# A four-layer graph network on one core: setup rebuilt, low rows split ahead of the turn, order set anew

## The reference

```python
def reference(x, adj, ...):                       # x: (32, 512, 256)
    x = _layernorm(x + _L0(x, adj, W, a))         # GAT, 1 head:  e = leaky(s1_i + s2_j), mask, softmax, @ h, elu
    x = _layernorm(x + _L1(x, adj, ...))          # 8 heads of 32: softmax(mask(q k^T / sqrt(32))) v, then FFN 256-256-256
    x = _layernorm(x + _L2(x, adj, W, a))         # GAT, 4 heads of 64
    x = _layernorm(x + _L3(x, adj, W1, W2, W3))   # e = leaky((x W1)(x W2)^T), mask, softmax, @ (x W3), relu
    return x
```

## Time and profile before

| | us |
|---|---|
| median of three executions | 3187.53 |
| profiled execution, its own time | 3182.73 |
| span in the profile | 3180.9 |
| PE busy | 2825.5 (89%) |
| ACT busy | 2719.1 (85%) |
| DVE busy | 2656.7 (84%) |
| POOL busy | 2497.8 (79%) |

### The profile page before, as it was taken

How to read it: one execution, slowest core, us unless ns; L and a number is a source line. 1 busy time by engine, 2 the same in 40 slices (tenths; PEclk the granted TensorE clock), 3 DMA queues, 4 the chain that set the end, 5 groups by cost and what they waited for, 6 DMA issues and landing times. The chain is left out here.

```text
span 3180.9 us, 69159 instructions
## 1 busy us (share of the span) xinstructions
PE 2825.5 (89%) x22342; PEld 1541.3 (48%) x22576; DVE 2656.7 (84%) x7357; ACT 2719.1 (85%) x5847; POOL 2497.8 (79%) x2521
## 2 busy tenths in 40 slices
PE   4899998998999999999989999998999999998855
PEld 3444444544555455554545454554454554454433
DVE  4878887988898799889888987988898798898774
ACT  4768888988898998898989879898898999897874
POOL 5657778878788787888878788887878887886874
PEclk8999999999999999999999999999999999999977
DMA  6435545755656666565656665574765566554454
GB/s 151 94 71 103 126 99 112 141 128 121 130 109 122 120 137 127 124 129 114 125 120 140 124 123 114 120 136 111 140 123 122 109 131 130 117 124 97 101 115 84
DMA packets 1215801, 378.88 MB, mean 119 GB/s; under 512 B 1157712, under 2 KB 1194320, under 8 KB 1215440
## 3 DMA queue, kind: packets, MB, share of 16 engines
q1 hardware_dynamic: 1213616, 373.46, 57.0%
q10 hardware_dynamic: 1824, 0.99, 0.2%
HBM read 21.43 MB, written 16.78 MB: 12 GB/s over the span
## 5 line engine op out<-in xcount | busy, mean ns | idle before, releaser
L855 POOL TENSOR_TENSOR split_r<-prob_r,split_r 128x512 f16<-128x512 f32 x768 | 929.7, 1222 | 219.8 <-DVE split_r L1299 219.8
L1264 DVE CUSTOM_DVE_ANT_0 unused<-bank_ps,neg_mask 128x512 bf16<-128x512 f32 x1024 | 650.2, 683 | 38.0 <-PE bank_ps L1466 34.9
L1531 PE MATMUL bank_ps<-val_r,trans_r 128*128 128x64 f16 (+1 forms) x9216 | 626.0, 221 | 58.6 <-DMA trans_r<-split_r 53.4
L1531 PEld LDWEIGHTS bank_ps<-val_r,trans_r 128*128 128x128 f16 x9216 | 523.4, 98 | 301.9 <-issue 109.4
L1084 ACT ACTIVATE prob_r<-bank_ps 128x512 f32<-128x512 f32 x1024 | 564.6, 597 | 120.9 <-remote 58.9
L1249 DVE CUSTOM_DVE_ANT_0 masked_r<-bank_ps,neg_mask 128x512 f32<-128x512 f32 x768 | 508.4, 681 | 130.7 <-ACT bank_ps L1050 102.6
L1299 DVE CAST split_r<-prob_r 128x512 f16<-128x512 f32 x768 | 537.3, 706 | 93.8 <-ACT prob_r L1062 78.6
L1062 ACT ACTIVATE prob_r<-masked_r,low_r 128x512 f32<-128x512 f32 x768 | 556.6, 734 | 53.0 <-DVE low_r L1249 38.3
L1491 PE MATMUL bank_ps<-prob_r,value_ones 128*64 128x512 f32 (+1 forms) x2048 | 553.9, 610 | 3.6 <-ACT prob_r L1084 2.0
L1482 PE MATMUL bank_ps<-stack 98*128 98x512 f16 x1024 | 394.2, 385 | 67.7 <-DVE low L1264 18.9
L861 POOL TENSOR_TENSOR split_r<-xcur,split_r 128x512 f16<-128x512 f32 x256 | 299.4, 1182 | 141.1 <-ACT split_r L976 140.6
(11 more groups left out here) (144 smaller groups left out, 4873.2 us busy)
## 6 DMA issues: line engine op xcount, KB each, us to landing
stack<-qk SPq DMA_DIRECT2D x384, 128.0 KB, 2.5
xcur<-in_x_dram SPq DMA_DIRECT2D x32, 512.0 KB, 5.0
out_dram<-z SPq DMA_DIRECT2D x32, 512.0 KB, 3.3
trans_r<-split_r SPq DMA_TRANSPOSE x768, 2.8
xt_r<-split_r SPq DMA_TRANSPOSE x320, 2.8
stack<-low_rows SPq DMA_DIRECT2D x128, 4.0 KB
qk<-in_adj_dram SPq DMA_DIRECT2D x1, 1024.0 KB, 8.1
z<-in_L_gnn_W_dram SPq DMA_DIRECT2D x4, 256.0 KB, 9.4
```

What stands on the lines that cost most here:

```text
L855: nc.gpsimd.tensor_tensor(split_r[:, j, 1, :], prob_r[:, i, :], split_r[:, j, 0, :], ALU.subtract).then_inc(lo_done.sem, 1)
L1264: nc.vector.tensor_tensor_reduce(out=unused[:, nth % 2, :], in0=bank_ps[entry("bank", "sq", g, t, b, h)][:], in1=neg_mask[:, b, :], scale= ...
L1531: ins = nc.tensor.matmul(bank[:, at:at + width], trans_r[:, i, pp, jb, :], val(g, layer)[:, vp, jb, cols], start=(n == 0), stop=(n == len( ...
```

## The change

**Setup.** The rows of graphs 0 and 1 are loaded among the first weights, and ACT and POOL split them (the list `EARLY`) ahead of most weights. The staging tiles move to other buffers (`STAGED`, slots 4 and 5, and `qk`), so that graphs 2 and 3 load without a wait. Five weights keep their low part on POOL (`SPLIT_POOL`), four get it on DVE (`SPLIT_DVE`) inside `later_setup`, which DVE runs just ahead of its first `mk`. PE waits for each weight where it is first used.

**Low rows.** `mh` on DVE is now three instructions in a chain of semaphores: the scaling, a cast to fp16, and a subtraction, all 128x16 and from SBUF to SBUF. `mt` turns high and low part together by four fp16 matmuls against an fp16 identity, into a bank of 8x512. `mr` casts all eight rows at once; `ml` is gone.

**Order.** `LATER` has new numbers for all kinds of tasks, and the costs of `mh` (0.22 to 0.45) and `mt` (0.4 to 0.25) in the planner are new.

```diff
-        "add_0": 60, "add_3": 66, "ap_0": 50, "ap_2": -3, "ap_ffn": -51, "bc": 22, "bt": -5, "dp": -40, "dv_2":
+    LATER = {"add_0": 28, "add_1": 13, "add_3": 110, "ap_0": 49, "ap_1": -4, "ap_2": 4, "ap_3": 30, "ap_ffn": -75, "ap_out": 41,
...
-            task(("mh", g, t), 0.22, [("mx", g, t, b, h) for b in range(NB) for h in range(QUAD)])
-            task(("mt", g, t), 0.4, [("mh", g, t)], opens=[("bank", ("mt", g, t))])
-            task(("mr", g, t), 0.49, [("mt", g, t)] + ([("md", g - 1, t)] if g else []))
-            task(("ml", g, t), 0.61, [("mr", g, t)], closes=[("bank", ("mt", g, t))])
-            task(("md", g, t), 1.0, [("ml", g, t), ("stack", g)], lands=2.2)
+            task(("mh", g, t), 0.45, [("mx", g, t, b, h) for b in range(NB) for h in range(QUAD)])
+            task(("mt", g, t), 0.25, [("mh", g, t)], opens=[("bank", ("mt", g, t))])
+            task(("mr", g, t), 0.49, [("mt", g, t)] + ([("md", g - 1, t)] if g else []),
+                 closes=[("bank", ("mt", g, t))])
+            task(("md", g, t), 1.0, [("mr", g, t), ("stack", g)], lands=2.2)
...
+        SPLIT_POOL = ("h0", "h2", "q", "k", "v")
+        SPLIT_DVE = ("f1", "f2", "h3", "g")
+        EARLY = [("x", g, 0, n) for g in range(2) for n in range(CT)]
+        STAGED = (4, 5)
...
             for kind, g, *key in ORDER["sp"]:
                 s = g % SLOTS
+                if (kind, g, *key) == ("xd", 2, 0, 0):
+                    sp.wait_ge(weights_lo, len(SPLIT_POOL))
+                    sp.wait_ge(setup_dve, 1)
+                    for staged_slot in STAGED:
+                        load(staged_slot)
                 if kind == "load":
                     if g >= SLOTS:
                         sp.wait_ge(*added.last((g - SLOTS, 3, p) for p in range(HALF)))
-                    elif g in (1, 2, 3):
-                        sp.wait_ge(weights_lo, W_SPLITS)
-                        sp.wait_ge(setup_dve, 1)
...
+            for _, g, phase, n in EARLY:
+                low_rows_of(g, phase, n)
+            for n, k in enumerate(SPLIT_POOL):
                 eng.wait_ge(weights_hi, n + 1)
                 nc.gpsimd.tensor_tensor(W[k][:, 1], scaled_weight(k), W[k][:, 0], ALU.subtract).then_inc(weights_lo, 1)
...
+                eng.wait_ge(rows_loaded, 80)
+                after(nc.vector.tensor_tensor(rows["fb2"][:], rows["fb2"][:], stage_b1, ALU.add))
+                for n, k in enumerate(SPLIT_DVE):
+                    eng.wait_ge(weights_hi, len(SPLIT_POOL) + n + 1)
+                    ins = nc.vector.tensor_tensor(W[k][:, 1], scaled_weight(k), W[k][:, 0], ALU.subtract)
+                ins.then_inc(setup_dve, 1)
...
                 elif kind == "mk":
                     unit = (g, *key)
+                    if (kind, *unit) == first_mask:
+                        later_setup()
...
                     nc.vector.scalar_tensor_tensor(out=low[s][:, t], in0=low[s][:, t], scalar=LOW_SCALE,
                                                    in1=some_col[:].unsqueeze(2).broadcast_to([P, NB, QUAD]),
-                                                   op0=ALU.mult, op1=ALU.mult).then_inc(low_scaled.sem, 1)
-                elif kind == "ml":
-                    t, = key
-                    dve.wait_ge(*low_rows_done.at(g, t))
-                    nc.vector.tensor_tensor(low_rows[:, 1, t, :], bank_ps[entry("bank", "mt", g, t)][0:QUAD, :],
-                                            low_rows[:, 0, t, :], ALU.subtract).then_inc(low_split.sem, 1)
+                                                   op0=ALU.mult, op1=ALU.mult).then_inc(low_chain, 1)
+                    low_links += 1
+                    dve.wait_ge(low_chain, low_links)
+                    parts = low_parts[s][:, t]
+                    nc.vector.tensor_copy(parts[:, :, 0, :], low[s][:, t]).then_inc(low_chain, 1)
+                    low_links += 1
+                    dve.wait_ge(low_chain, low_links)
+                    nc.vector.tensor_tensor(parts[:, :, 1, :], low[s][:, t], parts[:, :, 0, :],
+                                            ALU.subtract).then_inc(low_scaled.sem, 1)
...
                     for b in range(NB):
-                        ins = nc.tensor.transpose(bank[0:QUAD, b * P:(b + 1) * P], low[s][:, t, b, :], ident32[:])
+                        ins = nc.tensor.matmul(bank[0:2 * QUAD, b * P:(b + 1) * P],
+                                               low_parts[s][:, t, b].rearrange("p a h -> p (a h)"), ident16[:], start=True, stop=True)
```

More of the change, by code:

```diff
@@ L936, in scale_weight, with split_weight, high_rows_of @@
                 return nc.scalar.activation(stage_w[k], stage_w[k], ACT.Copy, scale=WSCALE)
+            def split_weight(k):
+                nc.scalar.copy(W[k][:, 0], scaled_weight(k)).then_inc(weights_hi, 1)
+            def high_rows_of(g, phase, n):
+                if phase == 0:
+                    act.wait_ge(*loaded(g))
+                else:
+                    for p in range(HALF):
+                        act.wait_ge(*applied.at(g, BEFORE_PHASE[phase], p))
+                was = prior("split", "x", g, phase, n)
+                if was is not None:
+                    act.wait_ge(*split_free(was))
+                nc.scalar.copy(cols_of(split_r[:, entry("split", "x", g, phase, n), 0, :]),
+                               rows_of(g, phase, n)).then_inc(rows_hi.sem, 1)
             eng.wait_ge(gat_loaded, 32)
             scale_weight("h0").then_inc(weights_scaled, 1)
-            eng.wait_ge(mh_loaded, 32)
-            scale_weight("h2").then_inc(weights_scaled, 1)
+            for _, g, phase, n in EARLY[:CT]:
+                high_rows_of(g, phase, n)
+            eng.wait_ge(weights_scaled, 1)
+            split_weight("h0")
             eng.wait_ge(dots_turned, 1)
@@ L944, in _ @@
                 nc.scalar.copy(t_tile, bank_ps[half][:].rearrange("p (t c) -> p t c", t=CT)).then_inc(dots_copied, 1)
+            eng.wait_ge(mh_loaded, 32)
+            scale_weight("h2").then_inc(weights_scaled, 1)
+            for _, g, phase, n in EARLY[CT:]:
+                high_rows_of(g, phase, n)
+            eng.wait_ge(weights_scaled, 2)
+            split_weight("h2")
+            eng.wait_ge(gram_done, 1)
+            nc.scalar.activation(stage_g, bank_ps[0][:].rearrange("p (t c) -> p t c", t=CT), ACT.Copy,
+                                 scale=WSCALE).then_inc(weights_scaled, 1)
             eng.wait_ge(qkv_loaded, 48)
@@ L947, in _ @@
                 scale_weight(k).then_inc(weights_scaled, 1)
+            eng.wait_ge(weights_scaled, 6)
+            for k in ("q", "k", "v"):
+                split_weight(k)
             eng.wait_ge(ffn_loaded, 80)
@@ L966, in _ @@
                 if kind == "x_hi":
-                    phase, n = key
-                    if phase == 0:
-                        act.wait_ge(*loaded(g))
-                    else:
-                        for p in range(HALF):
-                            act.wait_ge(*applied.at(g, BEFORE_PHASE[phase], p))
-                    was = prior("split", "x", g, phase, n)
-                    if was is not None:
-                        act.wait_ge(*split_free(was))
-                    nc.scalar.copy(cols_of(split_r[:, entry("split", "x", g, phase, n), 0, :]),
-                                   rows_of(g, phase, n)).then_inc(rows_hi.sem, 1)
+                    if ("x", g, *key) not in EARLY:
+                        high_rows_of(g, *key)
                 elif kind == "xt_hi":
@@ L1408, in _ @@
                     job, n = key
+                    if job != "c0":
+                        pe.wait_ge(weights_lo, 1 if job == "h0" else len(SPLIT_POOL))
+                    if job not in ("c0", "h0"):
+                        pe.wait_ge(setup_dve, 2)
                     for t in range(CT):
```

122 lines of the change are left out of this document (65 added, 57 removed), and 22 rows, old and new, of the table LATER.

## The result

Before and after ran side by side on one chip. The changed kernel takes **3154.78 us** (median of 4, 3148.64 to 3160.15), the kernel before 3185.7 us; the ratio is 0.9907, 95% interval 0.9891 to 0.9924. That is 31 us less, and 2 us from the 3157 that were forecast. The profiled execution took 3153.3 us, its span 3151.5, at a mean granted clock of 0.979 (before 0.969).

The account below looks back on a forecast made before the run. Four engines were taken to hold each other up, PE nearest its limit, so about half of PE savings count. Terms -19 - 11 + 18 - 16 = -28 gave 3155 for the profiled execution, 3157 us as median; range 3112 to 3205.

Parts of the forecast that it names:

- start: Setup: rows loaded early, first mask on DVE at 41 us instead of 60.13, -19 us (ends 13 and 23).
- order: New task order: a quarter of the 62 us in low-clock stretches is gained, -16 us.
- low rows, -11 + 18: Low rows: -11 us from cheaper fp16 turns on PE, +18 us from two more small DVE instructions ahead of `mt`.
- signs that I set down for right: First PE matmul 26 to 33 us, first mask 38 to 44, low-row matmuls 15 to 20, idle 70 to 90, among others.
- The rival by which half of the head start is given back: Start: transposes queue behind loads, late weights drag, order brings nothing; 3183 us, no change; chance 0.15.
- The rival that the rows come no earlier: Start: the DMA queue, not SP's wait, sets the first transpose; given no chance of its own.
- The low rows on PE: 256 fp32 transposes become fp16 matmuls, 17.7 us busy; PE saves 21.5 us, half reaches the end, -11 us.
- The low chain: DVE ahead of `mt`: 36 PE waits grow by 1.0 us each, half counts, +18 us (ends +6 and +80).
- my mark "below 50" for wrong: Idle time ahead of the low-row matmuls (L1534) below 50 us would show the prediction wrong.
- The slower rival: Low chain: POOL holds both new DVE instructions nearly every time, 64 sets grow by 2.0 us; 3217 us, chance 0.2.
- the bare stretch: Every third graph PE holds almost only `sq`, at low clock: 6.9 us each, some nine times, 62 us.
- the rival at 3125 us: Order: the low-clock stretch goes for good, three quarters of 62 us come through; chance 0.2.

Follow-up runs that it names:

- e1: Kernel before with the changed kernel's setup only, order and low rows old: 3173.0 us, ratio 0.9963.
- e8: Changed kernel with the low rows of before, `ml` put into DVE's row behind the planned end of `mr`: 3161.5 us, ratio 0.9924.
- after: The changed kernel itself: new setup, new order, new low rows with 3 links: 3154.8 us, ratio 0.9907.
- e4: Changed kernel with the setup of before, new order and new low rows kept: 3170.0 us, ratio 0.9951.
- e9: Kernel before with ten memsets on POOL ahead of its ninth weight split, to start the first graph late: median up 8.1 us, ratio 1.0024.
- e5: Kernel before with the new low rows cut to one DVE instruction per set, low part of the extremes left zero: 3180.8 us, ratio 0.9987.
- e6: Changed kernel with one DVE instruction per low-row set in place of three, low part of the extremes left zero: 3137.2 us, ratio 0.9853.
- e2: Kernel before with the new low rows (3 links), old setup, old order with `ml` struck out of DVE's row: 3243.7 us, ratio 1.0189.
- e7: Changed kernel with the cast made three times in a chain, so 5 links per set: 3194.6 us, ratio 1.0035.
- e3: Kernel before with new setup and new low rows (3 links), old order with `ml` struck out: 3227.8 us, ratio 1.0135.

## Why the prediction was right in its total, step by step

The total was right, and in part by luck. The split that e1, e8 and after give (setup, then order, then low rows) shows three terms that were each off by 4.5 to 13.7 us, with errors that cancelled:

| step | predicted us | measured on this path us |
|---|---|---|
| start | -19 | -11.5 |
| order | -16 | -11.5 |
| low rows, -11 + 18 | +7 | -6.7 |
| sum | -28 | -29.7 |

The two gains were 12 us smaller than forecast, and the loss that I forecast for the low rows did not come (each step is known to some 4 to 7 us). (The runs of before beside the changed kernel's own had a median of 3185.7 us, which is why the sum here is 29.7 and not 31.) Of the signs that I set down for right, PE's first matmul, the links' maxima and the fewer windows of low clock came. The first mask (45.00), the matmuls' 25.0 us, the links' means and the idle time did not.

**The start.** The turned rows came by the count of bytes: 29.60 us against "about 29". The first mask was forecast at 41 and came at 45.00, since I let `later_setup` begin at 33.5. I had left out that the second `ends` stands behind `val_r` in DVE's row, which waits for ACT until 36.58. I had counted all of it as carried to the end. From e4 to the changed kernel 14.4 us of the mask gave 15.2 of time, in the old order 17.6 gave 11.5 (e1) and 12.1 gave 8.1 (e9). Each of these shares is known to some 0.2 to 0.5, so that the new order carries more than the old is not shown. The rival by which half of the head start is given back and the order brings nothing (3183) fell by its time, but in the old order about a third does go. The rival that the rows come no earlier fell too: PE has them 24 us sooner.

**The low rows on PE.** Sized too high from two neighbours: the matmuls' busy time is 25.0 us and not 17.7, so 14.2 us are saved and not 21.5. The mean of 98 ns for 128 columns is nearer to the 123 of 256 columns than I had taken. Half of 14.2 is 7 us. With the further links removed, this saving and the loss of `ml` together are worth 3.7 us in the old order (before to e5) and 24 us in the new one (e8 to e6). My factor of one half is no constant of the kernel. I gave `ml`'s hop nothing; no run parts it from the matmuls.

**The low chain.** The term of +18 us met what e6 to after gives, +17.5 us, but its working was wrong, and this is luck. "PE already sits idle for this step 36 times, 45.4 us in all" misread the view: 31.5 of these us, 29 times, are idle time of the weight loads, and the matmuls waited 7 times, 13.9 us; the earlier trace rows had the 13.9. I then expected 36 waits to grow by 1.0 us each, to 81 us; it was 40.7, and my mark "below 50" for wrong was met. Nor does half of PE's idle time reach the end. From before to e2 the matmuls' part grew by 52.7 us and the time by 59, from e5 to e2 by 51.6 and 63, from after to e7 by 25.7 and 39.8, from e6 to after by 7.2 and 17.5: the time grew each time by more than the idle time ahead of these matmuls. The lost clock grew as well, by 8, 14, 12 and 4 us. Where a rest stays, no run shows what it is. The means were 0.28 and 0.27 us per link where I had taken 0.5, because the new order puts most sets where POOL has only small work.

**The slower rival** was priced at 64 sets x 2.0 us x 1/2 = 64 us. In the order of before it is near to what happened: e2 is 59 us slower, with 38 of 64 casts and 16 of 64 subtractions held, not all. I had put it at 0.2 from the median of L1270, "more than half of these are not held". But a median of the first link says nothing on the second: a held first link ends just as POOL takes its next instruction. By the page "SBUF — State Buffer" of the Trainium skill (section "Who interferes with whom") the port is a lock for the whole instruction and issue order decides who blocks. The pairs of ends above (1650.74 and 1650.78, 1651.86 and 1651.90) agree. POOL's L938, shown at the end, does not: it takes 1.04 us and holds nothing, and there the measurement decides.

**The order.** I priced it by the bare stretch alone, a quarter of 62 us, and its 6.9 us count some idle time twice: PE was busy 2.18 of the first 4 us at the low clock, so the clock cost 0.45 x 2.18 + 0.41 x 4 = 2.6 us and not 3.4. That stretch is real: in the kernels with the old order the clock falls at the same place in every third graph, here e1:

```profile
1310.00:1320.00 10.00, 6.31 (x44) 3.43 (x42) 9.46 (x32) 6.80 (x17) 7.04 (x7) 0.83 0.82 198
1600.00:1610.00 10.00, 8.45 (x54) 5.30 (x55) 9.91 (x27) 5.53 (x12) 7.03 (x7) 0.83 0.59 134
1880.00:1890.00 10.00, 5.59 (x30) 2.74 (x29) 9.54 (x28) 4.64 (x12) 7.77 (x7) 0.66 0.82 198
```

In the changed kernel the clock is under 0.99 at one place alone between 700 and 2800 us, from 1140 to 1160; its first window:

```profile
1140.00:1150.00 10.00, 7.40 (x54) 5.36 (x52) 8.91 (x28) 6.49 (x16) 4.98 (x4) 0.83 0.87 159
```

So the stretch went nearly for good, as the rival at 3125 us had it, and lost clock fell by 24 us (e1 to e8: 36), while the order as a whole gave 11.5 us. By the stores in the profiles of e1 and e8, the new order is 12.6 us late at the first graph, wins 18 us up to graph 25 and 11 us in the last graphs; that is 16.5 us in these two executions, since that of e8 took 5 us less than its median. I had named neither the fill nor the end. And the order, with the plan that knows the chain, is worth 73 us where the chain has three links: it is what keeps the low rows from being a loss. Terms that I added as if they were independent are not; with the low rows put ahead of the order, the same sum reads -11.5 (setup), +54.8 (low rows, e1 to e3), -73.0 (order, e3 to after). A table of runs that changes one part at a time from one end alone would have called the low rows a loss.

## What to carry to other kernels

Count the waits in a chain of small VectorE instructions that work from SBUF to SBUF, not their busy time: where GpSimd has long instructions in a row, each gap lets it take the next one, and the chain then moves at GpSimd's pace. Let independent instructions follow back to back, and wait once. Before pricing a wait, see which row of the profile it belongs to: idle time of the weight loads is not idle time of the matmuls. Where a fixed order repeats, a link is held in the same place each time, so price a new chain by what GpSimd does at that very place, and price an order and the code that it was set for together.

## What the hardware showed that I had not expected

- GpSimd held the chain only with its 128x512 tensor-tensor instructions. L938, a tensor-tensor of 128x4 that takes 1.04 us, held nothing: a link beside it took 0.16 to 0.17 us (after, 1713.87 to 1714.91 us). In all, 10 links of that run lay wholly inside one L938, and 19 of e7's, each at 0.16 to 0.18 us.

```profile
1713.87 1.04 POOL L938 TENSOR_TENSOR scale<-scale,exponent 128x4 f32<-128x4 f32 x1
...
1714.26 0.16 DVE L1322 SCALAR_TENSOR_TENSOR low<-low,some_col 128x16 f32<-128x16 f32 x1
...
1714.46 0.17 DVE L1328 CAST low_parts<-low 128x16 f16<-128x16 f32 x1
...
1714.67 0.17 DVE L1331 TENSOR_TENSOR low_parts<-low,low_parts 128x16 f16<-128x16 f32 x1
```

- A VectorE instruction that follows a held one back to back was not held by GpSimd's next (15 of 15 in the kernel before, and there GpSimd's instruction grew by 0.26 to 0.53 us), whereas one behind a semaphore, some 0.03 us later, was held 44 of 44 times (e2).
